# A two-part fp32 feed-forward and scan kernel: who computes the low parts of y1

## The chip, the cores and the metric

One core of one Trainium2 chip. The metric is device time in microseconds of one execution. Engines: PE is TensorE, PEld its weight loads, DVE VectorE, ACT ScalarE, POOL GpSimd, SP SyncE.

## The reference

The input x has 8 sequences of 512 tokens with 128 features. Three residual blocks follow one another:

```
x = x + 0.5 * ffn(layernorm(x))
x = x + attn(layernorm(x))
x = x + 0.5 * ffn(layernorm(x))

ffn(x):  h = silu(x @ w1.T * s1) * (x @ w2.T * s2)        # 128 -> 512
         h = gelu(h @ h1.T * sh1); h = gelu(h @ h2.T * sh2)  # 512 -> 512, exact gelu
         return h @ w3.T * s3                              # 512 -> 128
attn(x): h[t] = tanh(x[t] @ B + h[t-1] @ A.T)              # 16 states, 512 steps
         return (h @ C) @ W_out.T + b_out
```

The weights w1, w2, h1, h2, w3 are -1, 0 or 1; both ffn blocks use the same ones.

## The kernel before, in words

**Tiles.** The 4096 tokens are cut into 8 chunks of N = 512 columns; features lie on the 128 partitions. Each chunk goes through the feed-forward block twice, with the scan between, so there are 16 turns, 0 to 15; turn g handles feed-forward block g. Turns 0 to 5 are `early_turn`, 6 to 8 `middle_turn` (three of them, each with a scan chunk), 9 to 15 `turn`. The last scan runs beside turn 13; turn 14 has none, and turn 15 has no following block.

**Two parts.** A matmul takes operands of type fp32r. Every activation y is therefore split: a high part y_hi, the cast to fp32r, and a low part y_lo = y - y_hi. Each weight tile is multiplied with both, one matmul after the other (`split_mm`, line 222; the matmul is line 226). Weights have a low part only in a general case that these inputs don't need.

**A block.** Layer 1 has four pieces m = 0 to 3 of 128 hidden features. For each, TensorE fills two banks (with w1 and w2); ScalarE takes the tanh of one (line 816); VectorE forms u = (th + 1) * bank0 (line 583, called the u), y1 = bank1 * s * u (line 587, the product) and the cast y1_hi (line 593). Only for block 0, and its `late` form, does ScalarE make the cast (line 821). The low part of y1 is made by GpSimd (line 1010). Layers 2 and 3 have four output tiles each, of 8 matmuls; ScalarE applies gelu twice to each, once for y (line 834) and once for y_hi (line 837). Their low parts are shared: for y2 GpSimd makes parts 0 and 2, VectorE 1 and 3 (line 597); for y3 GpSimd makes part 0, VectorE 1 to 3. Layer 4 has one output tile, 4 groups of 2 matmuls; group k waits for y3's high and low part k.

**The order is written out by hand, per engine.** In turn g TensorE runs layer 2 of block g, then layer 1 of block g + 1 woven into layer 3 of block g, then layer 4: L2 (m = 0 to 3), L1 m = 0, 1, L3 m = 0, L1 m = 2, L3 m = 1, 2, L1 m = 3, L3 m = 3, L4 (in turns before 9: the same). Transposes for the layer norms and the eight scan steps stand between. The banks of layer 1 and layer 3 overlap: piece 2 of layer 1 uses F4 and F0 (`B1`), the third tile of layer 3 is F4 and the fourth F0 (`B3`). So line 298 waits for the third u of the next block ahead of the third tile, and line 300 for the third product ahead of the fourth.

VectorE in turn g, behind the layer-norm work: y2's low parts, then for layer 1 of block g + 1 u, product, cast for m = 0, 1, 2, then y3's low parts 1 and 2 (with the spread of the scan's states, line 619, between or behind them), then u, product, cast for m = 3, y3's low part 3, the attention's residual (line 627), layer 4's residual (line 611).

GpSimd in turn g: the inverse deviations (lines 1002, 1005), y2's low parts 0 and 2, y1's 0 of the next block, y3's 0, y1's 1, 2, 3.

Of the kernel before, what the change touches and what calls it, by code (L numbers as in the profile page):

```python
# [33 lines left out]
CHUNKS = 8  # L34
# [6 lines left out]
KT = HID // P  # L41
# [4 lines left out]
def wait(engine, sem, value):  # L46

    if isinstance(value, int) and value <= 0:
        return
    engine.wait_ge(sem, value)  # L50


def build(nc, xT, xtok, w1T, w2T, h1T, h2T, w3T, scales, AT, Bm, CTrep, WoutT, ident_d, mask_d, outT):
    with ExitStack() as ctx:
        def sb(name, shape, dt=F32):
            return ctx.enter_context(nc.sbuf_tensor(name, shape, dt))
# [4 lines left out]
        def sem(name):  # L61
            return ctx.enter_context(nc.semaphore(name))
# [58 lines left out]
        y1 = sb("y1", [P, KT, N])  # L121
        w_ne = y1[:, :, :].rearrange("p k n -> p (k n)")
        y23 = sb("y23", [P, KT, N])
        y1_hi = sb("y1_hi", [P, KT, N], F32R)
        y1_lo = sb("y1_lo", [P, KT, N], F32R)
# [49 lines left out]
        y1_hi_r = sem("y1_hi_r")  # L175
        y1_lo_r = sem("y1_lo_r")
        l2_mm = sem("l2_mm")
# [362 lines left out]
        def _(dve):  # L540
# [38 lines left out]
            def layer1(g, m, late=False):  # L579
                banks = (B1_LATE if late else B1)[m]  # L580
                dve.wait_ge(th_r, 4 * g + m + 1)
                wait(dve, y1_r, 4 * g + m - 1)
                nc.vector.scalar_tensor_tensor(out=u[:, m % 2, :], in0=th[:, m % 2, :], scalar=1.0, in1=banks[0][:, :],  # L583
                                               op0=ALU.add, op1=ALU.mult).then_inc(u_r, 1)
                dve.wait_ge(u_r, 4 * g + m + 1)
                wait(dve, y1_lo_r, 4 * g - 3 + m)
                nc.vector.scalar_tensor_tensor(out=y1[:, m, :], in0=banks[1][:, :], scalar=s12h[:, m:m + 1],  # L587
                                               in1=u[:, m % 2, :], op0=ALU.mult, op1=ALU.mult).then_inc(y1_r, 1)
                if late:
                    return  # L590
                dve.wait_ge(y1_r, 4 * g + m + 1)
                wait(dve, l2_mm, 4 * g)
                nc.vector.tensor_copy(y1_hi[:, m, :], y1[:, m, :]).then_inc(y1_hi_r, 1)  # L593

            def low(g, k, hi_r, y, y_hi, y_lo, out_sem):
                dve.wait_ge(hi_r, 4 * g + k + 1)
                nc.vector.tensor_tensor(y_lo[:, k, :], y[:, k, :], y_hi[:, k, :].bitcast(F32), ALU.subtract).then_inc(out_sem, 1)  # L597
# [48 lines left out]
            def early_turn(g, mid):  # L646
                xn_low(g + 1)
                if mid is not None:
                    middle_stats(mid)
                first_stats(g + 2)  # L650
                if mid is not None:
                    normalise("m", mid, MI, mv_m, rs_m, xnt_m)
                normalise("f", g + 2, cols(xt_all, g + 2), mv_f, rs_f, xnt_f)
                low(g, 1, y2_hi_r, y23, y2_hi, y2_lo, y2_lo_dve)
                low(g, 3, y2_hi_r, y23, y2_hi, y2_lo, y2_lo_dve)
                for m in range(KT - 1):
                    layer1(g + 1, m)
                low(g, 1, y3_hi_r, y23, y3_hi, y3_lo, y3_lo_dve)
                low(g, 2, y3_hi_r, y23, y3_hi, y3_lo, y3_lo_dve)
                layer1(g + 1, KT - 1)  # L660
                low(g, 3, y3_hi_r, y23, y3_hi, y3_lo, y3_lo_dve)
                if mid is not None:
                    own_xb(mid)
                layer4(0, g, g)
# [333 lines left out]
        @block.gpsimd  # L998
        def _(pool):
            def inverse_std(kind, g, mv, ve, rs):  # L1000
                pool.wait_ge(var[kind], g + 1)
                pool.tensor_tensor(ve[:, :], mv[:, :, 1], epsc[:, :], ALU.add).then_inc(veps[kind], 1)
                pool.wait_ge(veps[kind], g + 1)
                wait(pool, normed[kind], g)
                pool.tensor_tensor(rs[:, :], ve[:, :], mhalf[:, :], ALU.pow).then_inc(rstd[kind], 1)  # L1005

            def low(g, k, hi_r, per, y, y_hi, y_lo, out_sem, free):
                pool.wait_ge(hi_r, 4 * g + k + 1)
                wait(pool, *free)
                pool.tensor_tensor(y_lo[:, k, :], y[:, k, :], y_hi[:, k, :].bitcast(F32), ALU.subtract).then_inc(out_sem, 1)  # L1010

            def layer1(g, ms=range(KT)):
                for m in ms:
                    low(g, m, y1_hi_r, 4, y1, y1_hi, y1_lo, y1_lo_r, (l2_mm, 4 * g))

            def early_turn(g, mid):
                if mid is not None:
                    inverse_std("m", mid, mv_m, ve_m, rs_m)
                inverse_std("f", g + 2, mv_f, ve_f, rs_f)
                rest(g, True)  # L1020

            def middle_turn(g, c):
                if c > 0:
                    inverse_std("f", g + 1, mv_f, ve_f, rs_f)
                inverse_std("m", g - 1, mv_m, ve_m, rs_m)
                rest(g, True)

            def turn(k, g):
                last = isinstance(k, int) and k == CHUNKS - 1
                if not last:  # L1030
                    inverse_std("f", g + 1, mv_f, ve_f, rs_f)
                rest(g, not last)

            def rest(g, nxt):
                low(g, 0, y2_hi_r, 2, y23, y2_hi, y2_lo, y2_lo_pool, (l3_mm, 4 * g))
                low(g, 2, y2_hi_r, 2, y23, y2_hi, y2_lo, y2_lo_pool, (l3_mm, 4 * g))
                if nxt:
                    layer1(g + 1, range(1))
                low(g, 0, y3_hi_r, 2, y23, y3_hi, y3_lo, y3_lo_pool, (l4_mm, g))
                if nxt:  # L1040
                    layer1(g + 1, range(1, KT))


            pool.memset(a_blk[:, :], 0.0).then_inc(pool_set, 1)
            pool.wait_ge(set_up, 1)
            pool.wait_ge(ld_w[0], 16)
            pool.wait_ge(ld_w[1], 16)
            pool.wait_ge(w_hi_ready, 2)
            pool.tensor_tensor(w_lo[:, 0:WOFF[2]], w_raw[:, 0:WOFF[2]], w_hi[:, 0:WOFF[2]].bitcast(F32),
                               ALU.subtract).then_inc(w_lo1_ready, 1)  # L1050
            inverse_std("f", 0, mv_f, ve_f, rs_f)
            inverse_std("f", 1, mv_f, ve_f, rs_f)
            pool.wait_ge(ld_c, 48)
            for b in range(SEQS):
                i = pool.tensor_copy(b_rep[:, b, :], b_sb[:, :])
            i.then_inc(pool_set, 1)

            pool.wait_ge(gen_ready, 1)
            is_general = pool.value_load(general[0:1, 0:1], min_val=0, max_val=1)
            with pool.If(is_general != 0):  # L1060
                pool.tensor_tensor(w_lo[:, WOFF[2]:], w_raw[:, WOFF[2]:], w_hi[:, WOFF[2]:].bitcast(F32),
                                   ALU.subtract).then_inc(w_lo_ready, 1)
            layer1(0)
            early_turn(0, None)
            early_turn(1, 0)
            early_turn(2, 1)
            with pool.Fori(3, FIRST_PASS + 1) as k:
                early_turn(k, k - 1)
            middle_turn(CHUNKS - 2, 0)
            middle_turn(CHUNKS - 1, 1)  # L1070

            def round_(r):
                gb = r * CHUNKS
                if isinstance(r, int):
                    middle_turn(CHUNKS, 2)
                else:
                    inverse_std("f", gb + CHUNKS, mv_f, ve_f, rs_f)
                    layer1(gb + CHUNKS)
                    turn(0, gb + CHUNKS)
                turn(1, gb + 1 + CHUNKS)  # L1080
                with pool.Fori(2, CHUNKS - 2) as k:
                    turn(k, gb + k + CHUNKS)
                turn(CHUNKS - 2, gb + 2 * CHUNKS - 2)
                turn(CHUNKS - 1, gb + 2 * CHUNKS - 1)

            round_(0)
            pool.wait_ge(again_r, 1)
            need = pool.value_load(again[0:1, 0:1], min_val=0, max_val=1)
            with pool.If(need != 0):
                with pool.Fori(1, ROUNDS) as r:  # L1090
                    round_(r)
# [89 lines left out]
```

## Time and profile before

| | us |
|---|---|
| median of 3 runs | 451.89 |
| lowest, highest | 450.44, 452.21 |
| the profiled execution's own time | 449.82 |
| its span | 448.0 |
| granted TensorE clock over the span | 0.991 |
| TensorE matmul busy | 400.8 |
| VectorE busy | 325.5 |
| ScalarE busy | 234.7 |
| GpSimd busy | 193.5 |

All sums are made in times of the profiled execution, whose own time is 1.8 us more than its span. Matmuls overlap in the pipeline: a matmul of 512 columns is shown with some 0.39 us, but the next one starts about 0.23 us after it. So a late start is read from the starts.

### The profile page before, as it was taken

The numbers are of one execution on the slowest core, as the hardware profiler recorded it, in microseconds if no ns is written. First come the engines' busy times: TensorE is split into PE (matmuls) and PEld (weight loads), VectorE is DVE, ScalarE is ACT, GpSimd is POOL, SyncE is SP. The second block draws the span as 40 slices with busy tenths as digits, with TensorE's granted clock in tenths as the row PEclk, the third lists the DMA queues.
The fourth block names the chain that finished last, engine by engine and source line by source line (L and its number), as shares of the span: only waits on it lengthen the run. The fifth ranks groups of instructions, "written<-read, shape, count | busy, mean of one in ns | idle before, by whom it ended". The sixth has DMA issues, their size and how long they took to land.

```text
span 448.0 us, 6670 instructions
## 1 busy us (share of the span) xinstructions
PE 400.8 (89%) x1848; PEld 313.6 (70%) x1848; DVE 325.5 (73%) x672; ACT 234.7 (52%) x462; POOL 193.5 (43%) x174
## 2 busy tenths in 40 slices
PE   0458999999999999999989999999999999999881
PEld 0246777787878787786777768678686867877660
DVE  2475989999999989677778665949668594978521
ACT  3427646464655656454663546555363555646460
POOL 3246555444455545325344253535335253534420
PEclk9999999999999999999999999999999999999996
DMA  7900000000000000001001010010101001010001
GB/s 230 420 3 0 1 24 2 24 0 25 1 4 21 0 23 0 23 1 47 1 0 48 2 47 1 0 50 0 47 0 47 0 0 47 0 47 1 24 1 31
DMA packets 6046, 13.95 MB, mean 31 GB/s; under 512 B 1280, under 2 KB 1664, under 8 KB 5760
## 3 DMA queue, kind: packets, MB, share of 16 engines
q1 hardware_dynamic: 6016, 13.60, 8.1%
q8 instruction: 13, 0.21, 0.2%
q14 instruction: 17, 0.14, 0.1%
HBM read 7.30 MB, written 2.10 MB: 21 GB/s over the span
## 4 chain that ended last, share of the span: by engine, by line
PE 59%; DVE 19%; issue 12%; ACT 5%; POOL 2%; DMA 1%; DVEq 0%; SPq 0%; ACTq 0%; POOLq 0%
PE F L226 47%; DVE y_lo L597 4%; DVE y L587 4%; PE FR L226 4%; DVE u L583 4%; DVE y_hi L593 2%; PE SC L338 2%; ACT y_hi L837 2%; ACT th L816 1%; PE MI L323 1%; PE FR L245 1%; PE FR L255 1%; DVE xn_lo L577 1%; DMA w_raw<-in_w2T 1%; DVE h_wide L619 1%
## 5 line engine op out<-in xcount | busy, mean ns | idle before, releaser
L1010 POOL TENSOR_TENSOR y_lo<-y,y_hi 128x512 fp32r<-128x512 f32 x112 | 157.6, 1419 | 179.3 <-DVE y_hi L593 105.6
L226 PE MATMUL F<-y_hi,w_hi 128*128 128x512 f32 x512 | 213.7, 417 | 10.2 <-DVE y_lo L597 6.6
L226 PE MATMUL F<-y_lo,w_hi 128*128 128x512 f32 x512 | 200.9, 392 | 0.0
L834 ACT ACTIVATE y<-F,sc 128x512 f32<-128x512 f32 x112 | 77.0, 688 | 126.6 <-PE F L226 126.4
L226 PEld LDWEIGHTS F<-y_hi,w_hi 128*128 128x128 f32 x512 | 96.4, 188 | 38.5 <-issue 10.3
L226 PEld LDWEIGHTS F<-y_lo,w_hi 128*128 128x128 f32 x512 | 96.5, 188 | 18.5 <-issue 1.9
L597 DVE TENSOR_TENSOR y_lo<-y,y_hi 128x512 fp32r<-128x512 f32 x80 | 76.5, 964 | 40.1 <-ACT y_hi L837 39.7
L837 ACT ACTIVATE y_hi<-F,sc 128x512 fp32r<-128x512 f32 x112 | 76.6, 684 | 0.0
L816 ACT ACTIVATE th<-F,s1h 128x512 f32<-128x512 f32 x64 | 44.2, 690 | 33.5 <-PE F L226 21.8
L226 PE MATMUL F<-xn_hi,w_hi 128*128 128x512 f32 x127 | 55.3, 435 | 3.9 <-DVE xn_lo L577 3.3
L226 PE MATMUL F<-xn_lo,w_hi 128*128 128x512 f32 x127 | 50.8, 400 | 0.0
L587 DVE SCALAR_TENSOR_TENSOR y<-F,s12h,u 128x512 f32<-128x512 f32 x63 | 47.3, 751 | 3.6
L583 DVE SCALAR_TENSOR_TENSOR u<-th,F 128x512 f32<-128x512 f32 x64 | 43.5, 680 | 5.9 <-ACT th L816 5.7
L338 PEld LDWEIGHTS SC<-h_all,a_blk 128*128 128x128 f32 x208 | 38.1, 188 | 7.7
L593 DVE CAST y_hi<-y 128x512 fp32r<-128x512 f32 x60 | 35.7, 594 | 2.1
L853 ACT ACTIVATE h_all<-SC 128x8 f32 (+1 forms) x104 | 18.3, 176 | 28.7 <-PE SC L338 28.7
L226 PEld LDWEIGHTS F<-xn_hi,w_hi 128*128 128x128 f32 x127 | 24.4, 192 | 10.9 <-issue 2.3
L338 PE MATMUL SC<-h_all,a_blk 128*128 (+1 forms) x208 | 30.1, 217 | 0.0
L226 PEld LDWEIGHTS F<-xn_lo,w_hi 128*128 128x128 f32 x127 | 24.4, 192 | 4.9 <-issue 0.7
L226 PE MATMUL FR<-y_hi,w_hi 128*128 128x512 f32 x64 | 26.1, 407 | 0.0
L226 PE MATMUL FR<-y_lo,w_hi 128*128 128x512 f32 x64 | 25.1, 392 | 0.0
L571 DVE TENSOR_SCALAR xnt_f<-x_all,mv_f,rs_f 128x128 f32<-128x128 f32 (+1 forms) x32 | 19.6, 674 | 6.5 <-POOL rs_f L1005 6.5
(86 smaller groups left out, 313.0 us busy)
## 6 DMA issues: line engine op xcount, KB each, us to landing
x_all<-in_xT SPq DMA_DIRECT2D x1, 2048.0 KB, 15.0
x_all<-x1c SPq DMA_DIRECT2D x8, 256.0 KB, 2.2
x_all<-lnin SPq DMA_DIRECT2D x8, 256.0 KB, 2.3
out<-outb SPq DMA_DIRECT2D x8, 256.0 KB, 2.0
x_all<-in_xtok SPq DMA_DIRECT2D x1, 1792.0 KB, 10.7
w_raw<-in_h1T SPq DMA_DIRECT2D x2, 512.0 KB, 5.2
w_raw<-in_h2T SPq DMA_DIRECT2D x2, 512.0 KB, 6.8
x_all<-in_xtok SPq DMA_DIRECT2D x1, 256.0 KB, 2.9
```

What stands on the lines that cost most here:

```text
L226: mm = nc.tensor.matmul(out, wtile(w, layer, k, m), y, start=first and i == 0, stop=last and i == len(pairs) - 1)
L338: nc.tensor.matmul(SC[:, t * BLOCKS:(t + 1) * BLOCKS], a_blk[:, :], h_all[:, bass.ds(off, BLOCKS)], start=False, stop=t == CSTEPS - 1, ski ...
L571: i = nc.vector.tensor_scalar(out[:, q * P:(q + 1) * P], bankt[:, q * P:(q + 1) * P], mv[:, q, 0:1], rs[:, q:q + 1], ALU.subtract, ALU.mult)
L583: nc.vector.scalar_tensor_tensor(out=u[:, m % 2, :], in0=th[:, m % 2, :], scalar=1.0, in1=banks[0][:, :], op0=ALU.add, op1=ALU.mult).then_ ...
L587: nc.vector.scalar_tensor_tensor(out=y1[:, m, :], in0=banks[1][:, :], scalar=s12h[:, m:m + 1], in1=u[:, m % 2, :], op0=ALU.mult, op1=ALU.m ...
L593: nc.vector.tensor_copy(y1_hi[:, m, :], y1[:, m, :]).then_inc(y1_hi_r, 1)
L597: nc.vector.tensor_tensor(y_lo[:, k, :], y[:, k, :], y_hi[:, k, :].bitcast(F32), ALU.subtract).then_inc(out_sem, 1)
L816: nc.scalar.activation(th[:, m % 2, :], banks[m][0][:, :], ACT.Tanh, scale=s1h[:, m:m + 1]).then_inc(th_r, 1)
L834: nc.scalar.activation(y23[:, m, :], bankt[:, :], ACT.Gelu, scale=s)
L837: nc.scalar.activation(y_hi[:, m, :], bankt[:, :], ACT.Gelu, scale=s).then_inc(hi_r, 1)
L853: nc.scalar.activation(h_all[:, bass.ds(c * HCOLS + (t + 1) * BLOCKS, BLOCKS)], SC[:, t * BLOCKS:(t + 1) * BLOCKS], ACT.Tanh).then_inc(ste ...
L1010: pool.tensor_tensor(y_lo[:, k, :], y[:, k, :], y_hi[:, k, :].bitcast(F32), ALU.subtract).then_inc(out_sem, 1)
```

## The change

VectorE makes all four low parts of y1, each behind its cast. In the `late` form of block 0, where ScalarE casts, low part m - 1 stands behind product m, and the last one behind product 3. GpSimd loses its `layer1` function and every call of it; it keeps y2's parts 0 and 2, y3's part 0, and the inverse deviations. The semaphore y1_lo_r is now raised by VectorE; TensorE's waits on it (line 290) are unchanged, and the wait in front of the product has the same value written in another form.

```diff
@@ VectorE, layer1 @@
                 dve.wait_ge(u_r, 4 * g + m + 1)
-                wait(dve, y1_lo_r, 4 * g - 3 + m)
+                wait(dve, y1_lo_r, 4 * (g - 1) + m + 1)
                 nc.vector.scalar_tensor_tensor(out=y1[:, m, :], in0=banks[1][:, :], scalar=s12h[:, m:m + 1],
                                                in1=u[:, m % 2, :], op0=ALU.mult, op1=ALU.mult).then_inc(y1_r, 1)
                 if late:
+                    if m:
+                        low(g, m - 1, y1_hi_r, y1, y1_hi, y1_lo, y1_lo_r)
+                    if m == KT - 1:
+                        low(g, m, y1_hi_r, y1, y1_hi, y1_lo, y1_lo_r)
                     return
                 dve.wait_ge(y1_r, 4 * g + m + 1)
                 wait(dve, l2_mm, 4 * g)
                 nc.vector.tensor_copy(y1_hi[:, m, :], y1[:, m, :]).then_inc(y1_hi_r, 1)
+                low(g, m, y1_hi_r, y1, y1_hi, y1_lo, y1_lo_r)
@@ GpSimd @@
-            def layer1(g, ms=range(KT)):
-                for m in ms:
-                    low(g, m, y1_hi_r, 4, y1, y1_hi, y1_lo, y1_lo_r, (l2_mm, 4 * g))
...
-            def rest(g, nxt):
+            def rest(g):
                 low(g, 0, y2_hi_r, 2, y23, y2_hi, y2_lo, y2_lo_pool, (l3_mm, 4 * g))
                 low(g, 2, y2_hi_r, 2, y23, y2_hi, y2_lo, y2_lo_pool, (l3_mm, 4 * g))
-                if nxt:
-                    layer1(g + 1, range(1))
                 low(g, 0, y3_hi_r, 2, y23, y3_hi, y3_lo, y3_lo_pool, (l4_mm, g))
-                if nxt:
-                    layer1(g + 1, range(1, KT))
...
-            layer1(0)
             early_turn(0, None)
...
                     inverse_std("f", gb + CHUNKS, mv_f, ve_f, rs_f)
-                    layer1(gb + CHUNKS)
                     turn(0, gb + CHUNKS)
```

## Rows read from the trace of the kernel before

**Rows 1.** The page, part 1: busy us, share of the span, instructions.

```profile
PE 400.8 (89%) x1848; PEld 313.6 (70%) x1848; DVE 325.5 (73%) x672; ACT 234.7 (52%) x462; POOL 193.5 (43%) x174
```

**Rows 2.** Busy time in one early turn: stretch and length, busy us of each engine.

```profile
134.00:158.50 24.50, 24.47 (x120) 19.62 (x118) 22.87 (x47) 14.07 (x31) 12.29 (x11) 1.00 0.03 11
```

**Rows 3.** The waits, TensorE for VectorE: us in total, times, longest.

```profile
PE F L226 <- DVE y_lo L597: 6.6, 9, 1.7
```

**Rows 4.** Groups by line, VectorE: busy us, mean ns, idle before.

```profile
L597 DVE TENSOR_TENSOR y_lo<-y,y_hi 128x512 fp32r<-128x512 f32 x80 | 76.5, 964 | 40.1 <-ACT y_hi L837 39.7
...
L593 DVE CAST y_hi<-y 128x512 fp32r<-128x512 f32 x60 | 35.7, 594 | 2.1
```

**Rows 5.** Timeline of VectorE in turn 11: start us, us.

```profile
333.63 0.69 DVE L583 SCALAR_TENSOR_TENSOR u<-th,F 128x512 f32<-128x512 f32 x1
...
335.14 1.34 DVE L593 CAST y_hi<-y 128x512 fp32r<-128x512 f32 x1
336.40 1.78 DVE L597 TENSOR_TENSOR y_lo<-y,y_hi 128x512 fp32r<-128x512 f32 x1
338.10 1.78 DVE L619 TENSOR_TENSOR h_wide<-h_all,mask 128x512 f32<-128x512 f32 x1
339.81 0.68 DVE L597 TENSOR_TENSOR y_lo<-y,y_hi 128x512 fp32r<-128x512 f32 x1
340.41 0.67 DVE L583 SCALAR_TENSOR_TENSOR u<-th,F 128x512 f32<-128x512 f32 x1
341.12 0.75 DVE L587 SCALAR_TENSOR_TENSOR y<-F,s12h,u 128x512 f32<-128x512 f32 x1
341.90 0.43 DVE L593 CAST y_hi<-y 128x512 fp32r<-128x512 f32 x1
342.25 0.68 DVE L597 TENSOR_TENSOR y_lo<-y,y_hi 128x512 fp32r<-128x512 f32 x1
```

**Rows 6.** Timeline of TensorE in turn 11: layer 3's third tile, layer 4's last group.

```profile
334.91 0.47 PE L226 MATMUL F<-y_hi,w_hi 128*128 128x512 f32 x1
...
342.99 0.50 PE L226 MATMUL F<-y_hi,w_hi 128*128 128x512 f32 x1 [0.53 <-DVE y_lo L597]
```

**Rows 7.** Timelines of ScalarE (third cast part of y3, fourth tanh) and GpSimd, turn 11.

```profile
337.70 0.68 ACT L837 ACTIVATE y_hi<-F,sc 128x512 fp32r<-128x512 f32 x1
338.27 0.69 ACT L816 ACTIVATE th<-F,s1h 128x512 f32<-128x512 f32 x1
...
334.89 4.44 POOL L1010 TENSOR_TENSOR y_lo<-y,y_hi 128x512 fp32r<-128x512 f32 x3 [1.83 <-ACT y_hi L837]
```

**Rows 8.** Timelines of turns 0, 3 and 7: third u, third tile, turn 0's layer 4.

```profile
49.53 0.68 DVE L583 SCALAR_TENSOR_TENSOR u<-th,F 128x512 f32<-128x512 f32 x1
50.26 0.50 PE L226 MATMUL F<-y_hi,w_hi 128*128 128x512 f32 x1
50.52 4.42 POOL L1010 TENSOR_TENSOR y_lo<-y,y_hi 128x512 fp32r<-128x512 f32 x3 [1.38 <-ACT y_hi L837]
58.09 0.47 PE L226 MATMUL F<-y_hi,w_hi 128*128 128x512 f32 x1 [1.09 <-DVE y_lo L597]
...
121.96 0.69 DVE L583 SCALAR_TENSOR_TENSOR u<-th,F 128x512 f32<-128x512 f32 x1
123.03 0.47 PE L226 MATMUL F<-y_hi,w_hi 128*128 128x512 f32 x1
...
226.76 0.68 DVE L583 SCALAR_TENSOR_TENSOR u<-th,F 128x512 f32<-128x512 f32 x1
228.06 0.47 PE L226 MATMUL F<-y_hi,w_hi 128*128 128x512 f32 x1
```

**Rows 9.** Timelines of the start: fourth product of block 0, TensorE's fourth group of layer 2.

```profile
34.82 0.75 DVE L587 SCALAR_TENSOR_TENSOR y<-F,s12h,u 128x512 f32<-128x512 f32 x1
...
37.72 0.47 PE L226 MATMUL F<-y_hi,w_hi 128*128 128x512 f32 x1 [0.66 <-POOL y_lo L1010]
```

More of the change, by code:

```diff
@@ L1019, in early_turn @@
                 inverse_std("f", g + 2, mv_f, ve_f, rs_f)
-                rest(g, True)
+                rest(g)
             def middle_turn(g, c):
@@ L1025, in middle_turn @@
                 inverse_std("m", g - 1, mv_m, ve_m, rs_m)
-                rest(g, True)
+                rest(g)
             def turn(k, g):
@@ L1031, in turn @@
                     inverse_std("f", g + 1, mv_f, ve_f, rs_f)
-                rest(g, not last)
-            def rest(g, nxt):
+                rest(g)
+            def rest(g):
                 low(g, 0, y2_hi_r, 2, y23, y2_hi, y2_lo, y2_lo_pool, (l3_mm, 4 * g))
                 low(g, 2, y2_hi_r, 2, y23, y2_hi, y2_lo, y2_lo_pool, (l3_mm, 4 * g))
-                if nxt:
-                    layer1(g + 1, range(1))
                 low(g, 0, y3_hi_r, 2, y23, y3_hi, y3_lo, y3_lo_pool, (l4_mm, g))
-                if nxt:
-                    layer1(g + 1, range(1, KT))
             pool.memset(a_blk[:, :], 0.0).then_inc(pool_set, 1)
```

## The prediction

> **What bounds the kernel now.** I number the turns 0 to 15: six early ones (0 to 5), three middle ones (6 to 8), seven late ones (9 to 15). I read the page first: TensorE is busy 89% of the span, VectorE 73% [rows 1]. Then one early turn cut out by time: TensorE is busy in 24.47 of 24.50 us [rows 2], so there every delay of TensorE is a delay of the kernel. The list of waits says where TensorE does stand still later: mostly for a low part on VectorE, 6.6 us in nine waits, the longest 1.7 us [rows 3]. In the code that is the last low part of y3 ahead of the fourth group of layer 4. So there are two places to judge: the dense stretch of a turn, and its seam.
>
> The groups by line then show the contention: the low part on VectorE takes 964 ns in the mean, the cast 594 ns [rows 4]. The timeline of turn 11 resolves these means. A cast takes 0.43 us and a low part 0.68 us when GpSimd stands still, and 1.34 and 1.78 us beside GpSimd's run of three low parts (4.44 us), as does the spread of the states, 1.78 us [rows 5, 7]. GpSimd's run is y3's first low part and then y1's second and third. The chain on VectorE from the third cast to the last low part of y3 (335.14 to 342.93) is what TensorE waits for at 342.99 [rows 5, 6].
>
> **The change, part by part.** Removed from GpSimd: four low parts a turn. It keeps three, and none of these is later than before, as they stood ahead of or between the removed ones. Added to VectorE: four low parts per layer 1, 64 in all, 0.61 us each when issued back to back (339.81 to 340.41 in [rows 5]). No DMA moves, and SP's queue isn't touched. The wait in front of y1's product has the same value as before, and is now on VectorE's own work, so it costs nothing.
>
> What is gained: in turn 11 the third cast gives back 0.9 us, y3's low part and the spread 1.1 us each, together 3.1 us, all of it behind the third u. GpSimd's one remaining run, y3's first low part, starts at 334.89 and is over by about 336.2, before the third cast comes (below).
>
> What is paid ahead of the third u: a low part needs its cast finished. The cast ends 0.43 us after its start, and 0.03 us pass until a dependent instruction begins (product at 341.12 for 0.75 us, cast at 341.90); without a wait the next instruction begins 0.35 us after the cast (341.90 to 342.25) [rows 5]. So each low part costs 0.12 + 0.61 = 0.73 us, and the first two delay the third u by about 1.4 us. Its dependant is the third output tile of layer 3: its bank F4 is the one the third u reads, and TensorE waits for it ahead of that tile (line 298). That wait costs nothing now. Queued behind it on TensorE stands everything: layer 3's third tile, layer 1's fourth, layer 4.
>
> The slack there, from the end of the third u to the first matmul of the tile: in turn 11, 334.32 to 334.91, 0.59 us [rows 5, 6]; in turn 0, 50.21 to 50.26, 0.05; in turn 3, 122.65 to 123.03, 0.38; in turn 7, 227.44 to 228.06, 0.62 [rows 8]. With 0.06 us from release to start, the stall is 1.4 to 1.5 us in turn 0, 1.0 to 1.1 in turn 3, 0.8 to 0.9 in turns 7 and 11.
>
> How much comes back at the seam. ScalarE's third cast part of y3 ends at 338.38, 3.47 us after the third tile began [rows 6, 7]; nothing shortens this, and the fourth tanh behind it (0.69 us from 338.27) moves with it. Behind it VectorE has: y3's low part 0.6, u 0.7, product 0.8, cast 0.47, y1's low part 0.6, y3's last low part 0.68, with a start of 0.04: 3.9 us.
> - Turn 11: the tile starts 0.8 late at 335.7, so the last low part ends at 335.7 + 3.5 + 3.9 = 343.1 against 342.93. Cost 0.2 us: relief and stall nearly cancel. The first five late turns (9 to 13): 5 x 0.2 = 1.0.
> - Turn 0: tile at 51.7, end at 59.1, against 58.09, when layer 4 goes on now [rows 8]: 1.0 us. Turn 1 is built alike: 2.0 together.
> - Turn 3: TensorE has nearly no gap to give back [rows 2], so the stall stays whole: 1.0 us, in turns 2 to 5 together 4.0.
> - Turns 6 to 8: ScalarE interleaves its outputs with scan steps that follow TensorE, so they all move by 0.9; two low parts go into the tail (1.3 us) against less than 1 us of contention and spread. 3 x 0.9 = 2.7.
> - Turn 14 has late code but no scan beside it, so less slack; between 0.2 and 1.0, taken 0.6. Turn 15 has no layer 1: nothing.
> - The start: the first layer 1 is cast by ScalarE, and GpSimd makes the four low parts, on which TensorE waits until 37.72. The fourth product begins at 34.82 [rows 9]; with two low parts ahead of it, it ends 1.2 later at 36.8; ScalarE's cast 0.62 and the last low part 0.7 follow: 38.2 to 38.3. Cost 0.6.
>
> The sum is 0.6 + 2.0 + 4.0 + 2.7 + 1.0 + 0.6 = 10.9 us, on one core whose profiled execution took 449.82 us for a span of 448.0: 460.7. The median shown, 451.89, stands 2.1 us above it and would give 462.8. Three runs don't say which of the two a new measurement will stand on; I take the middle, 461.8.
>
> Bounds of the one price that no row shows directly, a low part behind its own cast. From below 0.61 us (no cost of the wait): 0.24 us less a turn, some 3 us in all over twelve stalling turns. From above, a wait that costs twice as much, 0.12 us more for each of the two: 3 us in all. I take 0.73, as the row of product and cast is the same engine and the same kind of wait.
>
> **A rule beside it.** By occupancy TensorE comes first, VectorE second; TensorE's weight loads are at 70%, below VectorE's 73% [rows 1]. The Trainium skill (Perfetto Trace Analysis, Identifying the Most-Contended Engine) wants TensorE judged by weight loads and not by matmuls, which makes VectorE the engine to relieve first. What that would make of the time is the second rival.
>
> **The rivals.**
> *Faster: the seam decides.* If the third u came in time, 3.1 us less on VectorE's chain would remove the waits for its low parts. Price: at most the 6.6 us of [rows 3], 451.9 - 6.6 = 445.3. It decides from the point where two low parts fit into the slack of 0.05 to 0.62 us; one already takes 0.61. Chance 0.06.
>
> *No change: VectorE's load decides.* 64 low parts at 0.61 us are 39 us more. Taken away are up to 80 x (0.96 - 0.68) = 22 us and 60 x (0.59 - 0.43) = 10 us [rows 4], and 8 x 1.1 = 9 us of spreads, as far as GpSimd's remaining run leaves them: about 0 net, and 452. For it: VectorE's share is large. Against it: its idle stretches lie in other places than the dense one. By the rule above this is the case. Chance 0.07.
>
> *Half: the early turns absorb it.* If VectorE reaches the first u sooner in the dense turns, turns 2 to 8 keep their time, and 10.9 - 6.7 = 4.2 is left: 456. Against it: the first u follows a tanh that follows TensorE. Chance 0.10.
>
> *More: the lost race.* In turn 0 the third u begins at 49.53; y1's second low part would begin 0.12 + 0.73 later, at 50.38, and GpSimd's first of y3 begins at 50.52 [rows 8]; turn 1 is alike. If GpSimd is first, the low part lasts up to 1.1 us longer, ahead of the third u: about 1 us more in two or three turns, and the same of the third cast elsewhere: 464 to 465. The cast of 1.34 us at 335.14 and the run that began at 334.89 [rows 5, 7] show that the later one waits. The Trainium skill (SBUF — State Buffer, Who interferes with whom) says so: whichever starts first has the port for the whole instruction; the trace agrees. Chance 0.13.
>
> Both places of the removed and the added work are in the diff, so I give no chance to a change that isn't made.
>
> **How the numbers follow.** The forecast has 0.64. The range reaches down to the half case and up to the lost race: 455.5 to 465.5, which leaves out 0.13 of the rivals and some of the forecast's own error. A measurement of this kernel tells about 0.5%, 2.3 us, from no change. Faster 0.06, within 0.07, slower 0.87.
>
> **What would show it.** Right: TensorE waits ahead of layer 3's third tile with a u of line 583 as the releaser, 0.8 to 1.5 us in turns 0 to 14, some 14 us in all; GpSimd's instructions of its low-part line fall from 112 to 48 and their mean to about 1.3 us; VectorE's cast has a mean near 0.45 us and its low part one near 0.7 us at 144; the last low part's wait at the seam stays near what it was in the late turns. Wrong: no wait for u, or an early turn that isn't longer, or low parts that still take over 1 us in the mean.

## The result, and the profile after

| | before | changed |
|---|---|---|
| median, us | 451.76 | 462.0 |
| lowest to highest | 450.44 to 452.21 | 460.83 to 462.49 |
| profiled execution, its span | 449.82, 448.0 | 462.49, 460.6 |

These are medians of four runs each. The ratio of changed to before is 1.0228, 95% interval 1.0199 to 1.0257: slower by 2.3%. The forecast was 461.8.

The page of the changed kernel, part 1, the line that answers to [rows 1]:

```profile
PE 403.4 (88%) x1848; PEld 316.3 (69%) x1848; DVE 333.4 (72%) x736; ACT 235.2 (51%) x462; POOL 98.6 (21%) x110
```

VectorE has 64 instructions more and only 7.9 us of busy time more; GpSimd has lost half of its own. By busy time the change is nearly free. The groups by line say why (they answer to [rows 4]; the line numbers have moved by 4 or 5):

```profile
L602 DVE TENSOR_TENSOR y_lo<-y,y_hi 128x512 fp32r<-128x512 f32 x144 | 96.6, 689 | 45.3 <-ACT y_hi L842 43.1
L1015 POOL TENSOR_TENSOR y_lo<-y,y_hi 128x512 fp32r<-128x512 f32 x48 | 62.7, 1308 | 158.8 <-ACT y_hi L842 158.8
L597 DVE CAST y_hi<-y 128x512 fp32r<-128x512 f32 x60 | 27.4, 456 | 2.1
```

The low part has fallen from 964 to 689 ns and the cast from 594 to 456: nearly all of the contention is gone. And yet the kernel is slower. The waits of TensorE, the view of [rows 3]: us in total, times, longest.

```profile
PE F L226 <- DVE u L583: 11.3, 15, 1.3
PE F L226 <- DVE y_lo L602: 6.6, 11, 1.2
```

The second line stands for the same 6.6 us as before, though not in the same turns: 0.53 us has become 0.30 in each of turns 10 to 13, and 1.67 has become 1.20 in turn 14, while turns 6 to 8, which had none, now have 0.75 each. The first line wasn't there before: 15 waits for a u, one in each of turns 0 to 14. Turn 11 shows one of them, VectorE first (as [rows 5]):

```profile
343.40 0.68 DVE L583 SCALAR_TENSOR_TENSOR u<-th,F 128x512 f32<-128x512 f32 x1
344.11 0.75 DVE L587 SCALAR_TENSOR_TENSOR y<-F,s12h,u 128x512 f32<-128x512 f32 x1
344.90 0.43 DVE L597 CAST y_hi<-y 128x512 fp32r<-128x512 f32 x1
345.36 0.69 DVE L602 TENSOR_TENSOR y_lo<-y,y_hi 128x512 fp32r<-128x512 f32 x1
345.97 0.68 DVE L583 SCALAR_TENSOR_TENSOR u<-th,F 128x512 f32<-128x512 f32 x1
346.79 0.75 DVE L587 SCALAR_TENSOR_TENSOR y<-F,s12h,u 128x512 f32<-128x512 f32 x1
347.57 0.43 DVE L597 CAST y_hi<-y 128x512 fp32r<-128x512 f32 x1
348.03 1.29 DVE L602 TENSOR_TENSOR y_lo<-y,y_hi 128x512 fp32r<-128x512 f32 x2
349.24 0.68 DVE L624 TENSOR_TENSOR h_wide<-h_all,mask 128x512 f32<-128x512 f32 x1
350.23 0.69 DVE L602 TENSOR_TENSOR y_lo<-y,y_hi 128x512 fp32r<-128x512 f32 x1 [0.30 <-ACT y_hi L842]
350.83 0.68 DVE L583 SCALAR_TENSOR_TENSOR u<-th,F 128x512 f32<-128x512 f32 x1
```

and TensorE, the two starts of [rows 6]:

```profile
346.70 0.50 PE L226 MATMUL F<-y_hi,w_hi 128*128 128x512 f32 x1 [0.59 <-DVE u L583]
...
354.14 0.50 PE L226 MATMUL F<-y_hi,w_hi 128*128 128x512 f32 x1 [0.30 <-DVE y_lo L602]
```

The third u ends at 346.65 and TensorE goes on at 346.70. Behind it every VectorE instruction has its short form, and at 350.23 VectorE even waits for ScalarE, whose work follows the late tile. From the tile to layer 4's last group it takes 7.44 us, against 8.08 in [rows 6]: the relief is real, and comes behind the stall.

To see where the time went, I cut each execution at the first u of each turn (line 583, every fourth one): us from cut to cut, in brackets the difference to the kernel before.

| stretch | before | changed | forecast |
|---|---|---|---|
| up to turn 0's first u | 45.84 | 48.63 (+2.8) | +0.6 |
| turns 0, 1 | 47.34 | 49.51 (+2.2) | +2.0 |
| turns 2 to 5 | 101.63 | 104.84 (+3.2) | +4.0 |
| turns 6 to 8 | 82.47 | 85.36 (+2.9) | +2.7 |
| turns 9 to 13 | 129.33 | 129.66 (+0.3) | +1.0 |
| turn 14 to the end | 41.39 | 42.60 (+1.2) | +0.6 |

### The profile page after: what moved, and what is told of

Same layout as the page of the kernel before. It is cut to its first block, busy times and chain, and to the rows that moved or that the text cites. A ratio compares the mean times of both kernels' runs of the same rounds, so it can differ in the third digit from the quotient of the medians.

```text
span 460.6 us, 6575 instructions
## 1 busy us (share of the span) xinstructions
PE 403.4 (88%) x1848; PEld 316.3 (69%) x1848; DVE 333.4 (72%) x736; ACT 235.2 (51%) x462; POOL 98.6 (21%) x110
## 4 chain that ended last, share of the span: by engine, by line
PE 39%; DVE 31%; issue 17%; ACT 6%; POOL 3%; DMA 1%; DVEq 1%; SPq 0%; ACTq 0%; POOLq 0%
PE F L226 33%; DVE u L583 8%; DVE y L587 7%; DVE y_lo L602 4%; DVE y_hi L597 4%; ACT y_hi L842 3%; DVE xnt_f L571 3%; DVE xnt_m L571 1%; ACT th L821 1%; PE MI L323 1%; POOL rs_m L1010 1%; PE SC L338 1%; PE FR L245 1%; PE FR L255 1%; DVE xn_lo L577 1%
## 5 line engine op out<-in xcount | busy, mean ns | idle before, releaser
L226 PE MATMUL F<-y_hi,w_hi 128*128 128x512 f32 x512 | 214.7, 419 | 22.0 <-DVE u L583 11.3
L602 DVE TENSOR_TENSOR y_lo<-y,y_hi 128x512 fp32r<-128x512 f32 x144 | 96.6, 689 | 45.3 <-ACT y_hi L842 43.1
L1015 POOL TENSOR_TENSOR y_lo<-y,y_hi 128x512 fp32r<-128x512 f32 x48 | 62.7, 1308 | 158.8 <-ACT y_hi L842 158.8
L597 DVE CAST y_hi<-y 128x512 fp32r<-128x512 f32 x60 | 27.4, 456 | 2.1
L1007 POOL TENSOR_TENSOR ve_f<-mv_f,epsc 128x4 f32<-128x4 f32 x16 | 3.2, 201 | 105.9 <-DVE mv_f L548 105.9
```

The lines of the kernel that those rows point to most:

```text
L226: mm = nc.tensor.matmul(out, wtile(w, layer, k, m), y, start=first and i == 0, stop=last and i == len(pairs) - 1)
```

## The experiments

Theories: *place*, the two low parts ahead of the third u make TensorE wait for the bank it reads; against it *load*, VectorE pays for 64 instructions wherever they stand. All edits are to the changed kernel but for the control. Medians are given with that of the kernel before on the same chip.

**1. The bank, not the order.** VectorE's order stays; layer 3's third tile goes to another bank, so TensorE waits for the second u.

```diff
-        B3 = [F[3], FR, F[4], F[0]]
-        B4 = F[1]
+        B3 = [F[3], FR, F[1], F[0]]
+        B4 = F[4]
...
                 if overlap and m == 2:
-                    pe.wait_ge(u_r, 4 * g + 7)
+                    pe.wait_ge(u_r, 4 * g + 6)
```

(In layer 1's `late` form the wait for layer 4's output moves from the third piece to the first, as F4 is used there.)

> The changed kernel, its VectorE order untouched, with another bank for layer 3's third tile: F1 instead of F4, and layer 4 in F4 instead of F1. TensorE then waits there for the second u and not for the third. Theory (the wait for bank F4): the stall is gone though the third u is as late as before, and the time is 450 to 453 us; what is left of the added work shows at the seam alone. Rival (VectorE's chain is late anyway, and the wait for the u only shows it earlier): the time lost moves to the last low part of y3, and it stays at 459 to 462 us.

Measured: 450.37 us, against 450.64 before on that chip: ratio 0.9985 (0.9959 to 1.0011). In turn 11 the third u and the tile now begin together; VectorE's and TensorE's timelines:

```profile
335.64 0.68 DVE L582 SCALAR_TENSOR_TENSOR u<-th,F 128x512 f32<-128x512 f32 x1
...
335.64 0.47 PE L226 MATMUL F<-y_hi,w_hi 128*128 128x512 f32 x1
```

The list of waits has none for a u left. What stays is at the seam:

```profile
PE F L226 <- DVE y_lo L601: 9.5, 12, 1.5
```

So the same instructions in the same order lose nothing against the kernel before once nobody waits for that bank. Load falls. The rival named there, that the loss only moves to the seam, falls too: the seam's waits rise by 2.9 us, while 11.3 us of waits for the u are gone. Nothing lost is a balance, though, and not a price of nothing: experiment 5 shows that the relief alone is worth 9.4 us, and what the low parts cost at the seam eats it up.

**2. The control: the swap without the change.** The same banks in the kernel before.

> Control: the kernel before with the bank swap alone, no low part moved. Theory (the swap only removes the wait for the third u, and that wait cost the kernel before nothing): within 0.3% of the kernel before, 449.5 to 452. Rival (the swap is worth something of its own, so what it gave beside the change says nothing of the stall): under 448 us.

Measured: 450.64 us, ratio to before 0.999 (0.9971 to 1.0009). The swap is worth nothing of its own.

**3. One low part ahead of the third u.**

```diff
-                low(g, m, y1_hi_r, y1, y1_hi, y1_lo, y1_lo_r)
+                for k in {0: (0,), 2: (1, 2), 3: (3,)}.get(m, ()):
+                    low(g, k, y1_hi_r, y1, y1_hi, y1_lo, y1_lo_r)
```

> The changed kernel with one low part of y1 ahead of the third u instead of two; the second and third stand behind the third cast. Theory (place): the third u is late by 0.73 us instead of 1.46, the waits for it fall to about 0.7 us in turns 0 and 1, 0.3 in 3 to 5, 0.1 in the middle and late turns, and the time is 451 to 453 us, nonlinear because the slack of 0.3 to 0.6 us now covers most of it. Rival (load): as without the move, 460 to 462; a cost linear in the low parts ahead of the third u would give the middle between it and the kernel with none ahead, about 455.

Measured: 451.92 us, ratio 1.0027 (1.0008 to 1.0046). The waits for a u fell from 11.3 us in 15 to 1.5 us in 3:

```profile
PE F L226 <- DVE u L583: 1.5, 3, 0.6
```

Half the delay costs an eighth of the waits for a u. That is slack being used up, 0.05 to 0.6 us a turn, and not a price per instruction.

**4. None ahead: the first three behind the third cast.** As in 3, with `{2: (0, 1, 2), 3: (3,)}`.

> The changed kernel with the first three low parts of y1 moved behind the third cast; VectorE still makes all four, so its load is that of the changed kernel. Theory (place): the stall of TensorE ahead of layer 3's third tile (11.3 us in 15 waits) is gone, the contention with GpSimd stays away, and the time is 448 to 450 us, a little under the kernel before. Rival (load): 64 more instructions on VectorE cost what they cost wherever they stand, and it stays at 459 to 462 us.

Measured: 458.9 us, ratio 1.0152 (1.0105 to 1.0199). This expectation was wrong in its time, and in that the contention stays away. The waits for a u are gone as expected, but those for a low part have more than doubled:

```profile
PE F L226 <- DVE y_lo L603: 14.4, 16, 2.0
```

Turn 11's VectorE shows the two things that I had not summed:

```profile
340.08 1.23 DVE L597 CAST y_hi<-y 128x512 fp32r<-128x512 f32 x1
341.24 2.49 DVE L603 TENSOR_TENSOR y_lo<-y,y_hi 128x512 fp32r<-128x512 f32 x4
343.64 0.68 DVE L625 TENSOR_TENSOR h_wide<-h_all,mask 128x512 f32<-128x512 f32 x1
344.25 0.68 DVE L603 TENSOR_TENSOR y_lo<-y,y_hi 128x512 fp32r<-128x512 f32 x1
344.85 0.68 DVE L583 SCALAR_TENSOR_TENSOR u<-th,F 128x512 f32<-128x512 f32 x1
```

and GpSimd's one remaining run there:

```profile
339.74 1.29 POOL L1016 TENSOR_TENSOR y_lo<-y,y_hi 128x512 fp32r<-128x512 f32 x1 [7.50 <-ACT y_hi L843]
```

The third cast is early again, so it falls on GpSimd's low part of y3 and takes 1.23 us; in the changed kernel it came after it. Then the three low parts stand, 1.8 us, in the chain that ends at the seam. The fourth u begins 5.10 us after the third tile (339.75), against 5.50 before and 4.13 in the changed kernel. Behind it y1's fourth low part adds 0.7 us, and layer 4's last group begins 8.41 us after the tile (348.16), against 8.08 before and 7.44 in the changed kernel. So there are two places where a low part costs, ahead of the third u and between it and the seam.

The seams don't account for all of this run. Cut as in the table above, its execution is 9.3 us longer than that of the kernel before: 4.3 in turns 0 to 13 and 0.3 at turn 14's seam, which is the cost of the place; 1.6 at the start, where the granted clock is low near 38 us as in experiments 9 and 10 below; 1.5 between layer 4's last residual and the end; and 1.6 behind turn 14's seam. There TensorE stood for 2.0 us, and behind that its mean clock from 426 to 430 us was 0.57, with matmuls up to 0.43 us apart instead of 0.23. TensorE's timeline, and busy time by engine with the clock in the third column from the end:

```profile
425.32 0.47 PE L226 MATMUL F<-y_hi,w_hi 128*128 128x512 f32 x1 [2.03 <-DVE y_lo L603]
...
426.00:430.00 4.00, 4.00 (x13) 3.15 (x13) 0.80 (x2) 0.24 (x1) 0.00 (x0) 0.57 0.17 66
```

The four times are 459.15, 458.96, 458.83 and 455.83 us; whether the last lacked such a stretch isn't shown. For VectorE's same instructions the time is 458.9 here, 451.9 in 3 and 450.4 in 1. It is place once more that decides, only not one place, and about half of what this execution loses is no wait for a low part.

**5. The removal alone.** As 4, and each of VectorE's low parts of y1 for blocks 1 to 15 cut to 8 of 512 columns; the rest of them is left out.

```diff
-                    low(g, k, y1_hi_r, y1, y1_hi, y1_lo, y1_lo_r)
+                    dve.wait_ge(y1_hi_r, 4 * g + k + 1)
+                    nc.vector.tensor_tensor(y1_lo[:, k, 0:8], y1[:, k, 0:8], y1_hi[:, k, 0:8].bitcast(F32),
+                                            ALU.subtract).then_inc(y1_lo_r, 1)
```

> The removal alone: GpSimd makes no low part of y1, and VectorE makes 8 of its 512 columns, behind the third and fourth cast; the low parts of y1 for blocks 1 to 15 are left out but for these columns. Theory: what the removed contention is worth when nothing is paid for it, at the seams of turns 0, 1, 6 to 8 and 9 to 14: 442 to 446 us. Rival (GpSimd's removed work was hidden): 450 to 452 us.

Measured: 441.28 us, ratio 0.9787 (0.9756 to 0.9817), 0.7 us below the expected range. The removed work was worth 9.4 us: that is what a good place for the low parts can win. The casts still take 584 ns in the mean here, since the third one is early and falls on GpSimd's low part of y3 as in 4. The seam's waits:

```profile
PE F L226 <- DVE y_lo L605: 2.7, 6, 0.8
```

**6. The fourth low part out of the seam, the stall left in.** It moves behind y3's last low part in the early turns, behind the attention's residual in the others.

```diff
-                low(g, m, y1_hi_r, y1, y1_hi, y1_lo, y1_lo_r)
+                if m < KT - 1:
+                    low(g, m, y1_hi_r, y1, y1_hi, y1_lo, y1_lo_r)
...
                 if att is not None:
                     attention(att[0], att[1])
+                if not last:
+                    low(g + 1, KT - 1, y1_hi_r, y1, y1_hi, y1_lo, y1_lo_r)
                 layer4(1, g, k)
```

> The changed kernel in its own banks, with y1's fourth low part moved behind y3's last low part (early turns) or behind the attention's residual (the others), and nothing else. Theory: the stall for the third u (11 us in 15 waits) stays, the 0.6 us at each of about ten seams goes: 455 to 457 us. The two costs add. Rival (the seam of the changed kernel is set by TensorE's late third tile alone, so the fourth low part was hidden): 460 to 462.

Measured: 455.92 us, ratio 1.0105 (1.0066 to 1.0144). The two costs stand side by side: the waits for a u keep their size when those for a low part fall, against the changed kernel's 11.3 and 6.6 us:

```profile
PE F L226 <- DVE u L583: 11.4, 15, 1.3
...
PE F L226 <- DVE y_lo L603: 2.0, 3, 0.8
```

**7. The same, with one ahead of the third u.**

> One low part ahead of the third u, two behind the third cast, the fourth moved behind as in the run beside; banks as in the kernel before. Theory: the run with one ahead had 451.9; less 0.6 us at eleven seams, 445 to 447 us, so without the bank swap most of the gain is to be had by order alone. Rival (without the swap the third u still holds TensorE, or the two low parts behind the third cast set the seam): 449 to 452.

Measured: 445.14 us, ratio 0.9858 (0.982 to 0.9897): by order alone, in the banks of the kernel before, the change becomes 1.4% faster.

**8. The swap of 1 and the move of 6 together.**

> The bank swap, and besides y1's fourth low part moved out of the seam: behind y3's last low part in the early turns and behind the attention's residual in the others. What is left of the added work then stands in front of nothing that TensorE waits for. Theory (place): 0.6 us off each seam that waits for VectorE, twelve of them, and 442 to 445 us, 1.3 to 2% under the kernel before. Rival (the next thing in line is as late, y3's high part from ScalarE or the transposes of the next turn): 448 to 451 us.

Measured: 441.61 us against 451.42 before, ratio 0.9794 (0.9768 to 0.982): faster than both kernels, by 2.1% than the one before. It computes all low parts and is as fast as run 5 without them (ratio 0.9787). The 0.4 us below the expected range is the size of the spread (440.58 to 442.27). Turn 11's seam, VectorE:

```profile
334.44 0.75 DVE L586 SCALAR_TENSOR_TENSOR y<-F,s12h,u 128x512 f32<-128x512 f32 x1
335.23 0.43 DVE L596 CAST y_hi<-y 128x512 fp32r<-128x512 f32 x1
335.57 0.69 DVE L602 TENSOR_TENSOR y_lo<-y,y_hi 128x512 fp32r<-128x512 f32 x1
336.17 0.75 DVE L632 SCALAR_TENSOR_TENSOR lnin<-MI,sc,x_all 128x512 f32<-128x512 f32 x1
336.83 0.68 DVE L602 TENSOR_TENSOR y_lo<-y,y_hi 128x512 fp32r<-128x512 f32 x1
337.43 0.74 DVE L616 SCALAR_TENSOR_TENSOR outb<-F,s3h,x_all 128x512 f32<-128x512 f32 x1
```

y1's low part now stands at 336.83, between two residuals; TensorE's waits for a low part are down to

```profile
PE F L226 <- DVE y_lo L602: 2.2, 3, 0.8
```

**9. The start on GpSimd again**, in the changed kernel:

```diff
                 if late:
-                    if m:
+                    if m and not isinstance(g, int):
                         low(g, m - 1, y1_hi_r, y1, y1_hi, y1_lo, y1_lo_r)
-                    if m == KT - 1:
+                    if m == KT - 1 and not isinstance(g, int):
                         low(g, m, y1_hi_r, y1, y1_hi, y1_lo, y1_lo_r)
...
+            for m in range(KT):
+                low(0, m, y1_hi_r, 4, y1, y1_hi, y1_lo, y1_lo_r, (l2_mm, 0))
             early_turn(0, None)
```

> The changed kernel, but the four low parts of block 0, at the start, are made by GpSimd again. Theory (VectorE's two low parts ahead of the fourth product cost 0.6 us, and the longer standstill of TensorE that they make brings on a stretch of about 4 us at the lower granted clock, 0.5, near 38 us): both go, and it gains 1 to 2.5 us on the changed kernel, 459.5 to 461 where that has 462. Rival (the stretch at the lower clock comes from elsewhere and stays): 0.5 us or nothing.

**10. The same in the kernel of 8.**

> The bank swap, the fourth low part behind, and block 0's low parts on GpSimd again. Theory: a further 1 to 2 us under the run with swap and move alone, 441 to 443.5 us, and no stretch at a clock of 0.5 near 38 us. Rival: the same time as that run.

Measured: 460.09 us (459.29 to 462.76) in 9, 441.02 (439.82 to 443.06) in 10. Against the kernel before on the same chip that is 1.0222 (1.0187 to 1.0256), as the changed kernel's 1.0228, and 0.9784 (0.9754 to 0.9815), as the 0.9794 of 8: the 1 to 2 us more that I expected can't be told. The cuts tell more than the medians. From the first u of block 0 to that of turn 0 it takes 18.86 us in the kernel before and 18.94 in run 9; with the low parts on VectorE, 19.42, 19.44 and 19.41 in runs 3, 5 and 8. Run 10, with the start on GpSimd, has 19.17. So the start costs 0.2 to 0.6 us. Runs 4 and 1, the changed kernel and runs 7 and 6 have 20.50, 20.60, 20.91, 20.89 and 21.02. These larger figures go with a granted clock of 0.5 for part of 37 to 42.5 us; of the changed kernel and run 9, busy time by engine with the clock in the third column from the end:

```profile
38.00:42.00 4.00, 3.74 (x9) 2.73 (x10) 2.56 (x12) 3.21 (x5) 1.15 (x2) 0.59 0.00 0
```

```profile
38.00:42.00 4.00, 4.00 (x18) 3.27 (x18) 2.56 (x11) 2.63 (x5) 2.46 (x3) 1.00 0.00 0
```

The part of the expectation that blamed VectorE's two low parts for this stretch does not hold. The control of run 2 has the start of the kernel before, takes 20.48 us for it, and shows the stretch too:

```profile
38.00:42.00 4.00, 4.00 (x12) 3.09 (x12) 2.44 (x9) 1.60 (x3) 2.45 (x3) 0.57 0.00 0
```

## Why the prediction was right

The forecast was a stall ahead of layer 3's third tile that the relief behind it only partly gives back, and both came as described. The instructions came out as named: GpSimd's low parts 48 at 1308 ns, VectorE's 144 at 689, its casts at 456.

**The stall.** Its term was 0.73 us per low part ahead of the third u. In turn 11 the cast at 344.90 is followed by the low part 0.46 us later and by the u 0.61 us after that; without a low part the u came 0.34 us after the cast: 0.46 + 0.61 - 0.34 = 0.73, as forecast. TensorE's waits are 11.3 us where I wrote some 14: this column counts from the matmul's shown end, about 0.16 us after the next could have started, and 15 times 0.16 is 2.4.

**Turns 0 and 1**: 2.2 us for 2.0. **Turns 2 to 5**: 3.2 for 4.0; turn 2 alone took 0.5 instead of 1.0, since its third u had already waited 0.37 us for a tanh, and the other three 0.85 to 0.95. I had costed all four like turn 3. For turn 3 I had also read "nearly no gap to give back" from a busy time of 24.47 in 24.50 us, and there the row hides something. A matmul is shown with 0.39 us and the next can start after 0.23, so a delay under 0.16 us doesn't show at all. At turn 3's seam the kernel before has

```profile
130.41 0.39 PE L226 MATMUL F<-y_lo,w_hi 128*128 128x512 f32 x1
130.64 0.50 PE L226 MATMUL F<-y_hi,w_hi 128*128 128x512 f32 x1
130.98 0.39 PE L226 MATMUL F<-y_lo,w_hi 128*128 128x512 f32 x1
131.43 0.47 PE L226 MATMUL F<-y_hi,w_hi 128*128 128x512 f32 x1
131.74 0.39 PE L226 MATMUL F<-y_lo,w_hi 128*128 128x512 f32 x1
```

with starts up to 0.45 us apart, and experiment 5 makes this turn 0.4 us shorter, turns 2 to 5 together 1.5. The changed kernel gave next to none of it back, so the term held all the same. **Turns 6 to 8**: 2.9 for 2.7. **Turns 9 to 13**: 0.3 for 1.0; relief and stall cancel more fully than summed, 0.1 a turn and -0.1 in turn 9. **Turn 14 and the end**: 1.2, of which 0.9 by turn 14's seam (12.49 to 13.36 us from its first u to layer 4's last group), where I took 0.6 between bounds of 0.2 and 1.0. **The start**: 0.2 to 0.6 us for 0.6; the other 2.2 to 2.6 in the table are 0.7 before block 0's first u, where the change touches nothing, and the rest goes with the stretch at the lower clock.

**The sum.** 10.9 us forecast; between the profiled executions 12.6 us of span, between the medians 10.2. Without the 2.2 us or more at the start that the change didn't cause, the stretches add up to 10.4 or less. That the forecast of 461.8 lies 0.2 us from the median is partly luck: the late turns and turn 2 came out lower, the middle turns and turn 14 higher, and the base was a middle between two that lie 2.1 us apart.

**The rivals.** *The seam decides* fell: its condition, a third u in time, isn't met in the changed kernel. It is met in experiment 4 and not needed in experiment 1, and the one takes 1.5% more than the kernel before, the other as long, since the added low parts stand in the seam's chain. The 9.4 us of experiment 5 show that the relief I had priced at 6.6 us at most was larger. Its listed waits for a low part fall by 3.9 us, from 6.6 to 2.7, and those of the attention's matmuls for h_wide by 1.8, from 2.7 to 0.9 (those of their weight loads from 6.9 to 2.2); 1.5 us come from turns 2 to 5, where the list has no such wait. The rest isn't placed. *VectorE's load decides* forecast a busy time about as before (39 us more and up to 41 less); measured were 7.9 us more, since some 31 went. That the kernel's time rose by 10.2 us beside it could still look like load. But over the kernels with all 64 low parts on VectorE the two don't go together: 330.8 us busy and 441.6 of time (experiment 8), 332.2 and 455.9 (6), 332.4 and 450.4 (1), 332.8 and 445.1 (7), 333.4 and 462.0 (the changed kernel), 334.3 and 451.9 (3), 339.6 and 458.9 (4). *The early turns absorb it* fell with turns 2 to 8, +6.1 us. *The lost race* did not happen. In turn 0 of the changed kernel y1's second low part begins 0.15 us ahead of GpSimd's run, and it is GpSimd's that is long, 1.68 us:

```profile
53.16 0.69 DVE L602 TENSOR_TENSOR y_lo<-y,y_hi 128x512 fp32r<-128x512 f32 x1
...
53.31 1.68 POOL L1015 TENSOR_TENSOR y_lo<-y,y_hi 128x512 fp32r<-128x512 f32 x1 [5.76 <-ACT y_hi L842]
```

In experiment 4 it is the other way round: in turn 11 GpSimd's low part begins first, at 339.74, keeps its 1.29 us, and VectorE's cast, 0.34 us behind it, takes 1.23 instead of 0.43. The Trainium skill (SBUF — State Buffer, Who interferes with whom) says that issue order decides who blocks; these two runs show it.

## What to carry to other kernels

Here the work moved to an engine with idle time cost what it delayed, not what it took. For each added instruction find the next instruction on that engine whose result another engine waits for, and the slack of that wait: the same 64 instructions gave 441.6, 450.4, 458.9 and 462.0 us by their order and by one bank. When a tile's bank is released late, another bank may be cheaper than another order (441.6 us in 8 against 445.1 in 7), and a low part that is needed a turn later belongs behind everything that is needed now. A busy share near 1 doesn't show that an engine loses nothing; the distances between its starts do.

## What the runs showed of the hardware

The spread of one kernel's times goes in part with the granted clock. Of 17 executions of the kernel before beside experiments 2, 8, 9 and 10, the seven with a mean granted clock of 0.991 to 0.995 have a median of 450.1 us, the ten with 0.978 to 0.982 one of 451.9; the two groups overlap (up to 452.73 in the first, down to 449.89 in the second). The profiles show the lower clock, 0.5 or 1.2 GHz, at the start: in the changed kernel it is 0.50 from 26 to 30 us, 0.76 from 30 to 34 and 0.59 from 38 to 42, in the kernel before 1.0 from 26 to 48. TensorE stands still between its matmuls there, but how long it was busy just before doesn't tell the profiles apart. Between 34 and 38 us it was busy for 1.72 of 4 us in the changed kernel and 2.60 in the control of experiment 2, which then have 0.59 and 0.57, and for 1.55 in experiment 3, 1.66 in 5 and 2.42 in the kernel before, which then have 1.0. What decides it in one execution stays open.

A dependent instruction on VectorE begins 0.03 us after the end of the one that it waits for, while one without a wait begins about 0.07 us ahead of that end (0.61 us after the start of a low part of 0.68, against 0.71 from u to product). So a wait on one's own result costs 0.1 us even where nothing else is late.
